# A tile's block sums: their low part one chunk earlier, TensorE's wait for it two products later, and columns laid out with the feature halves outermost

## What is computed

```python
def _dense(x, wi_, wo_):
    return jax.nn.relu(x @ wi_) @ wo_      # 256 -> 1024 -> 256
s0 = _dense(x, swi[0], swo[0])             # two experts shared by all samples
s1 = _dense(x, swi[1], swo[1])
h  = relu(x @ wi[type_label]); eo = h @ wo[type_label]   # a sample's own, one of five
w  = softmax(relu(gate_in @ g1) @ g2)      # gate_in: row 0 of eo, s0, s1
x  = x + eo * w[:, 0] + s0 * w[:, 1] + s1 * w[:, 2]
x  = x + zX * lap_x + zY * lap_y + zR * x * (1 - x)      # second differences along both axes
```

## Time and profile before

| | us |
|---|---|
| median of 3 executions (1141.07 to 1141.55) | 1141.53 |
| the profiled execution's own time | 1140.22 |
| its span | 1138.6 |
| TensorE matmuls busy in the span (98%, 6472 instructions) | 1115.2 |
| VectorE busy (69%) | 784.0 |
| ScalarE busy (49%) | 557.3 |
| granted TensorE clock, mean | 1.0 |

### The profile page before, as it was taken

One profiled execution on the slowest core, in us unless ns is written; L12 is line 12 of the kernel. 1 busy time (PEld: TensorE's weight loads), 2 busy tenths in 40 slices (PEclk: granted clock), 3 DMA queues, 4 the chain that ended last, 5 costly groups with the idle time before them and its releaser, 6 DMA issues.

```text
span 1138.6 us, 18531 instructions
## 1 busy us (share of the span) xinstructions
PE 1115.2 (98%) x6472; PEld 975.4 (86%) x6472; DVE 784.0 (69%) x1305; ACT 557.3 (49%) x1086; POOL 86.1 (8%) x127
## 2 busy tenths in 40 slices
PE   9999999999999999999999999999999999999998
PEld 8888888888888888888898888888888888888888
DVE  5655666666675645786776777867867778678666
ACT  3554655556555423364454454543644545545433
POOL 2111212112111002000000000000000000000001
PEclk9999999999999999999999999999999999999999
DMA  8655656556565323112123023021131130220300
GB/s 268 177 165 179 193 173 209 166 183 184 168 208 167 110 69 106 33 61 77 25 60 85 17 68 84 12 75 39 50 81 23 62 85 15 71 66 28 76 29 24
DMA packets 111806, 112.99 MB, mean 99 GB/s; under 512 B 78473, under 2 KB 87266, under 8 KB 111714
## 3 DMA queue, kind: packets, MB, share of 16 engines
q1 hardware_dynamic: 97282, 60.69, 19.4%
q0 software_dynamic: 13952, 50.60, 14.1%
q10 hardware_dynamic: 480, 0.53, 0.2%
HBM read 90.44 MB, written 17.04 MB: 94 GB/s over the span
## 4 chain that ended last, share of the span: by engine, by line
PE 97%; issue 2%; DVE 1%; DMA 1%; ACT 0%; POOLq 0%; POOL 0%; DVEq 0%
PE acc L1303 30%; PE acc L1304 15%; PE hbank L1175 11%; PE hbank L1176 11%; PE hbank L1174 11%; PE hbank L1230 3%; PE hbank L1231 3%; PE hbank L1232 3%; PE tbank L1231 1%; PE tbank L1230 1%; PE tbank L1232 1%; PE acc L1212 1%; DMA rw<-in_L_cond_wo 1%; PE acc L1080 0%; PE acc L1287 0%
## 5 line engine op out<-in xcount | busy, mean ns | idle before, releaser
L1303 PE MATMUL acc<-swo,hh 128*128 128x512 f32 x992 | 359.9, 394 | 0.0
L1417 ACT ACTIVATE hh<-hbank 128x512 fp32r<-128x512 f32 (+1 forms) x304 | 169.5, 560 | 362.0 <-PE hbank L1176 358.8
L811 DVE SCALAR_TENSOR_TENSOR hl<-hbank,hh 128x512 fp32r<-128x512 f32 (+1 forms) x304 | 194.4, 641 | 218.6 <-ACT hh L1417 218.5
L1304 PE MATMUL acc<-swo,hl 128*128 128x256 f32 x992 | 277.6, 280 | 0.0
L1303 PEld LDWEIGHTS acc<-swo,hh 128*128 128x128 f32 x992 | 186.2, 188 | 35.6
L1304 PEld LDWEIGHTS acc<-swo,hl 128*128 128x128 f32 x992 | 187.0, 189 | 6.2
L1303 PE MATMUL acc<-ewo,hh 128*128 128x512 f32 x496 | 180.1, 395 | 0.4 <-DVE hl L811 0.4
L1304 PE MATMUL acc<-ewo,hl 128*128 128x256 f32 x496 | 138.9, 280 | 0.0
L1176 PE MATMUL hbank<-xh,swl 128*128 128x512 f32 (+1 forms) x304 | 116.8, 384 | 0.0
L1175 PE MATMUL hbank<-xl,swh 128*128 128x512 f32 (+1 forms) x304 | 116.4, 383 | 0.0
L1174 PE MATMUL hbank<-xh,swh 128*128 128x512 f32 (+1 forms) x304 | 115.5, 380 | 0.0
(11 more groups left out here) (299 smaller groups left out, 1922.1 us busy)
## 6 DMA issues: line engine op xcount, KB each, us to landing
rw<-in_L_cond_wi POOLq DMA_DIRECT2D x44, 512.0 KB, 4.4
rw<-in_L_cond_wo POOLq DMA_DIRECT2D x44, 512.0 KB, 4.8
eo_scratch<-eo SPq DMA_DIRECT2D x128, 64.0 KB, 2.4
xs<-in_x SPq DMA_DIRECT2D x16, 512.0 KB, 4.3
rw<-in_x SPq DMA_DIRECT2D x256, 32.0 KB, 2.1
ei<-eo_scratch SPq DMA_DIRECT2D x16, 512.0 KB, 5.5
xs<-in_x SPq DMA_DIRECT2D x126, 64.0 KB, 3.5
out<-ot SPq DMA_DIRECT2D x15, 512.0 KB, 6.2
```

Source lines behind the costliest of these rows:

```text
L811: e.scalar_tensor_tensor(h_slot(HL, g), bank[:, 0:w], 0.0, h_slot(HH, g).bitcast(F32), ALU.max, ALU.subtract).then_inc(h_lo, 1)
L1303: e.matmul(acc[j][:, 0:2 * D], HH[:, g % NH, at], woc[:, f, :], start=(c == 0), stop=False)
L1304: m = e.matmul(acc[j][:, D:2 * D], HL[:, g % NH, at], woc[:, f, 0:D], start=False, stop=last)
L1417: e.activation(h_slot(HU if upright(g) else HH, g), bank_of(g)[:, 0:w], ACT.Relu).then_inc(h_hi, 1)
```

## The change

Three edits. `column_sums_low` goes from chunk 7 of the even pass to chunk 6, behind `result`. TensorE's waits for it and for the weight sums go from the first of the three products of chunk 0 to the third. And the forms `XH`, `XL`, `TH`, `TL` are laid out "k j n": feature half outermost, so that `tile_cols` and `half_block` pick one run of 512 or 256 columns. `XZ` stays "j k n", so the four instructions that go from `XZ` to such a form now step through `XZ` in another order than they write (`by_half`, `cut_view`).

```diff
+        def by_half(a):
+            return a.rearrange("p (j k n) -> p k j n", j=4, k=2)
+        def cut_view(a):
+            return a.rearrange("p (k j n) -> p k j n", j=4, k=2)
         def half_block(a, k, h):
-            return a.rearrange("p (j k n) -> p j k n", j=4, k=2)[:, 2 * h:2 * h + 2, k, :]
+            return a[:, (2 * k + h) * 256:(2 * k + h + 1) * 256]
...
         def tile_cols(a, k):
-            return a[:].rearrange("p (j k n) -> p j k n", j=4, k=2)[:, :, k, :]
+            return a[:].rearrange("p (k j n) -> p k j n", j=4, k=2)[:, k, :, :]
...
             def tile_low_whole(t):
-                e.tensor_tensor(XL[tile % 2][:], XZ[:], XH[tile % 2][:].bitcast(F32), ALU.subtract).then_inc(xt_lo, 1)
+                e.tensor_tensor(cut_view(XL[tile % 2][:]), by_half(XZ[:]), cut_view(XH[tile % 2][:]).bitcast(F32),
+                                ALU.subtract).then_inc(xt_lo, 1)
...
             def column_sums_low(t):
-                e.tensor_tensor(TL, XZ[:], TH.bitcast(F32), ALU.subtract).then_inc(ts_lo, 1)
+                e.tensor_tensor(cut_view(TL), by_half(XZ[:]), cut_view(TH).bitcast(F32), ALU.subtract).then_inc(ts_lo, 1)
...
-                    if b == 0 and seven(n + 1) and c == 7:
-                        column_sums_low(t)
...
                         if c == 6:
                             result(t - 1)
+                            if seven(n + 1):
+                                column_sums_low(t)
...
                 def product(to, hi, lo, cols, start, stop):
-                    to = to.rearrange("p (j n) -> p j n", n=128)
...
                     if c == 0:
                         e.wait_ge(*low_done(prev - 3))
-                        e.wait_ge(ts_lo, SEVENS.index(n) + 1)
-                        e.wait_ge(dve_seq, AT["weight sums"])
...
                     if c == 0:
                         e.wait_ge(*low_done(prev - 1))
+                        e.wait_ge(ts_lo, SEVENS.index(n) + 1)
+                        e.wait_ge(dve_seq, AT["weight sums"])
                     else:
                         e.wait_ge(p_sum, 3 * q - 1)
                     of_sum(other, 3, y[0][1], True, False).then_inc(h_prod, 1)
```

More of the change, by code:

```diff
@@ L674, in tile_low_whole @@
                 e.wait_ge(xt_hi, t + 1)
-                e.tensor_tensor(XL[tile % 2][:], XZ[:], XH[tile % 2][:].bitcast(F32), ALU.subtract).then_inc(xt_lo, 1)
+                e.tensor_tensor(cut_view(XL[tile % 2][:]), by_half(XZ[:]), cut_view(XH[tile % 2][:]).bitcast(F32),
+                                ALU.subtract).then_inc(xt_lo, 1)
             def column_sums(t):
-                x = [[half_block(XZ[:], k, h) for h in range(2)] for k in range(2)]
+                x = [[by_half(XZ[:])[:, k, 2 * h:2 * h + 2, :] for h in range(2)] for k in range(2)]
                 e.wait_ge(xt_lo, t + 1)
@@ L1408, in tile_high_whole @@
                 e.wait_ge(h_prod, END[LAST_PASS[tile - 2]])
-                e.activation(XH[tile % 2][:], XZ[:], ACT.Copy).then_inc(xt_hi, 1)
+                e.activation(cut_view(XH[tile % 2][:]), by_half(XZ[:]), ACT.Copy).then_inc(xt_hi, 1)
             def hidden_high(g):
@@ L1422, in column_sums_high @@
                     e.wait_ge(h_prod, END[FIRST + 2 * t - 1])
-                e.activation(TH, XZ[:], ACT.Copy).then_inc(ts_hi, 1)
+                e.activation(cut_view(TH), by_half(XZ[:]), ACT.Copy).then_inc(ts_hi, 1)
             def weight_sums_high():
```

## The result

| | before | changed |
|---|---|---|
| median, us (lowest to highest, 4 executions each) | 1141.3 (1140.1 to 1141.55) | 1120.24 (1119.25 to 1120.99) |
| the profiled execution | 1140.22 | 1120.99 |
| its span | 1138.6 | 1119.4 |

The ratio is 0.9817, with a 95% interval of 0.98 to 0.9834: 1.8% faster, 21 us between the medians. The forecast was 1121.5 with a range of 1119.7 to 1125.0.

A forecast was written before the change was run, and what follows sets the result against it. TensorE, its matmuls busy 98% of the span, was taken to bound the kernel. Terms of -20.0 us for 14 stalls, 0 for the moved wait and 0 for the layout took 1141.53 to 1121.5 us; range 1119.7 to 1125.0.

The forecast's parts named there:

- the stall: TensorE's wait at the first matmul of each of 14 seven-product odd passes, 1.2 us each, 16.8 in all; ended by `ts_lo`.
- issue: Cause the view of waits gave at line 1230, taken as no releaser found because three semaphores stand ahead of that matmul.
- The price, 1.43 us a pass: Gain per odd pass at its first matmul: 1.36 us of gap plus 0.07 of restart; 14 passes give 20.0 us.
- restart of 0.07: After the stall the odd pass's second matmul follows after 0.19 us instead of 0.12, another 0.07 per pass.
- The 0.04 us: Cost of a wait released with nothing to spare, read at chunk 1; 0.6 us over 14 passes, kept for the range.
- The room at the third product, 0.23 us: Chunk 7's low part would be ready 0.23 us before the third product's weight load, so the moved wait costs nothing.
- The layout at nothing: New column layout costs or gains zero in VectorE and ScalarE conversions and in TensorE's matmuls.
- The bound of 1.5 us: TensorE operands in one run instead of runs of 128: at most 0.01 us per chunk slower, 152 chunks, 1.5 us.
- a rival: One run of columns is cheaper on TensorE; 0.05 us a chunk would gain 7.6 us, giving 1113.9; chance 3 in 100.
- The first rival: Stall returns at the third product; a subtraction twice as long costs 13.9 us, giving 1135.4; chance 8 in 100.
- the last rival: Slower than before: subtraction over 2.4 times as long; at three times 10.8 us lost, giving 1152.3; chance 2 in 100.
- The 0.47 us a pass, 6.6 us in all: Wait said to remain at the odd pass's start without the first two products' 0.70 us of cover.

The follow-up runs named there:

- the kernels with VectorE put back: Changed kernel plus VectorE work between block sums' low part and chunk 7's: one 128x128 instruction 1120.58 us, three 1125.73, subtraction done twice 1134.54.
- the kernel with three small instructions: Changed kernel plus three scratch 128x128 VectorE instructions between the block sums' low part and hidden chunk 7's: 1125.73 us, ratio to before 0.9868.
- the second subtraction: Changed kernel with the block sums' low part computed twice in chunk 6, same result: 1134.54 us, ratio to before 0.9945.

## Why the prediction was right

- **What ended the stall.** I read it off one coincidence, a VectorE end 0.06 us ahead of a weight load. It was no accident: in the trace of before the distance is 0.06 or 0.07 at all 14 places. The two kernels with one edit each show the cause: the gap went where `ts_lo` and the wait for the weight sums went, and it vanished when the subtraction alone was moved. The reason I gave for the name "issue", three semaphores ahead of the matmul, doesn't hold: the kernels with VectorE put back have the same three ahead of the third product, and there the view names the releaser (`DVE hl`). Why it names that one and not the subtraction isn't known.
- **The price, 1.43 us a pass.** Measured on the weight loads 1.44, in all 20.2 for 20.0. The matmul's restart of 0.07 was rightly part of this sum, since I had counted the gap from matmul start to matmul start. Carried over to the price of a new wait, in the expectation of the kernel with three small instructions, it was counted beside the lateness of the weight load, which holds it already. The 0.04 us that I read from chunk 1 as the price of a wait with nothing to spare looks like such a lateness too. There, in the timeline of before, a weight load of line 1304 starts at 529.24 and that of the waiting matmul at 529.52, 0.28 us apart where 0.23 is usual behind such a load: 0.05 late. No run here tests that place by itself.
- **The room at the third product, 0.23 us.** The trace after has 0.32 - 0.06 = 0.26. The kernels with VectorE put back bear this out: 0.21 us cost nothing, 0.61 cost 0.34 a pass and the second subtraction, 1.27, cost 1.00, each time what goes beyond the 0.26, to 0.01.
- **The layout at nothing.** Shown by itself on TensorE, VectorE and ScalarE. The bound of 1.5 us, which I had kept for the range, was no property of the runs. The rule of the Trainium skill's "Advanced Engine Details and Errata", section "PSUM Cachelines", from which I made a rival, didn't show for an operand in runs of 128: 8.34 us for three chunks in either layout. The operand lies in SBUF, while the section is about PSUM, and no run here varies the pattern of a matmul's output in PSUM, so the rule isn't tested there.
- **The first rival.** Its price was right, 13.9 us forecast for a subtraction of twice the length and 14.0 measured, but its condition didn't come about. Nor did that of the last rival, a subtraction slower still.
- **What I passed over.** I said that the cover of the moved wait is the first two products. That is so, but I didn't ask whether the wait had to be moved at all. By the same timeline the subtraction would end 0.14 us before even the first product's load, and the kernel with that edit alone has the whole gain. The 0.47 us a pass, 6.6 us in all, that I put down as what would be left without the cover belong to chunk 7's low part, which only the third product needs; it ends 0.32 us ahead of its load with the wait moved and 0.31 with the subtraction moved alone. So they are not what moving the wait is worth. Once the subtraction is in chunk 6, the moved wait adds nothing to be measured, and the layout adds nothing at all; the moved wait only leaves the subtraction more room. Without the subtraction's move it is worth 9.8 us.
- **The rest of the difference.** The measured median lies 1.3 us under the forecast and inside the range. Of this 0.2 is the median of before, 1141.3 where I had started from 1141.53, and the rest a difference of 21.1 instead of 20.0. In the profiled executions the 14 stalls explain the spans to 0.1 us, together with the 0.86 us at the start. That the medians came out 0.9 us further apart than 20.2 is within their interval (18.9 to 22.8 us by the ratio) and has no shown cause.

## What to carry to other kernels

Where an engine that is 98% busy shows the same small idle time once per tile, line up the end of each candidate with the next weight load; the same few hundredths of a microsecond between them at every place point at the releaser even where the view of waits doesn't, and a kernel with that one instruction moved shows it. Then lay the releasing engine's order out anew with its real durations and see what its next result is late for: here a swap of two instructions was worth 20 us, with 0.26 us of room left behind it. Before a wait is moved too, ask of the same timeline whether it would still be late where it stands. And price a wait on TensorE by how late its weight load comes against the usual distance, neither by the matmuls' idle time, which was too little in each of these kernels, nor with a restart on top.

## What was not expected of the hardware

- A wait of TensorE can be missing from the matmuls' waits and still cost time: at 0.34 us per pass, 4.8 us in all, only the weight loads showed it (3.8 us, 14 times). The matmuls' idle time reported 16.8 us for a loss of 20.2, 10.1 for one of 14.0 and 6.8 for one of 10.4. The weight loads' idle time is nearer, but not exact either: 20.8, 13.0, 9.3 and 3.8 us for 20.2, 14.0, 10.4 and 4.8.
- The wait at the third product, met 0.11 us before the weight load was due, cost nothing, and met too late it cost its lateness, 0.34 or 1.00 us, with nothing on top. In each late case the load started 0.05 to 0.07 us after VectorE's end.
